# Unread products of constants on TensorE between the last expert pair and the first attention stream

## What is computed

```python
x = x + tanh(g_xattn[0]) * L0_xattn(layernorm(x), ctx)
x = x + tanh(g_ffn[0]) * L0_ffn(layernorm(x))      # 64 routed experts, top 4, and 2 shared ones
x = x + tanh(g_xattn[1]) * L1_xattn(layernorm(x), ctx, ctx)   # 32 query heads of 8, 8 key heads
x = x + tanh(g_ffn[1]) * L1_ffn(layernorm(x))      # causal attention of 16 heads, then gate, up, down
...
```

## Time and profile before

| | us |
|---|---|
| median of 3 launches | 1212.7 (1212.69 to 1216.48) |
| the profiled launch, its own time | 1211.12 |
| its span, first to last instruction | 1209.3 |
| TensorE busy | 1038.0 (86%) |
| VectorE busy | 722.9 (60%) |
| ScalarE busy | 523.0 (43%) |
| GpSimd busy | 308.2 (25%) |

### The profile page before, as it was taken

How to read it: one execution, slowest core, us unless ns; L and a number is a source line. 1 busy time by engine, 2 the same in 40 slices (tenths; PEclk the granted TensorE clock), 3 DMA queues, 4 the chain that set the end, 5 groups by cost and what they waited for, 6 DMA issues and landing times.

```text
span 1209.3 us, 18846 instructions
## 1 busy us (share of the span) xinstructions
PE 1038.0 (86%) x6621; PEld 660.5 (55%) x6621; DVE 722.9 (60%) x1630; ACT 523.0 (43%) x881; POOL 308.2 (25%) x618
## 2 busy tenths in 40 slices
PE   6399999999999788887889899962566978999997
PEld 4378888888887333333556337342223434556575
DVE  6965544544447568767655124487796665684744
ACT  3332222222243676665545411334553644544643
POOL 3024343434435555335331200010312200000000
PEclk9589999999999789899999999995767889999999
DMA  5202111121450000000000300020000000000000
GB/s 147 54 14 51 41 45 46 41 50 39 121 161 1 1 3 3 2 2 3 2 3 4 122 1 1 0 53 0 1 2 1 3 2 1 1 10 1 9 9 10
DMA packets 62461, 32.10 MB, mean 27 GB/s; under 512 B 47121, under 2 KB 61089, under 8 KB 62129
## 3 DMA queue, kind: packets, MB, share of 16 engines
q1 hardware_dynamic: 62384, 31.10, 9.6%
HBM read 29.64 MB, written 1.05 MB: 25 GB/s over the span
## 4 chain that ended last, share of the span: by engine, by line
PE 74%; DVE 17%; ACT 4%; issue 3%; POOL 1%; DMA 1%; POOLq 0%; DVEq 0%; SPq 0%; ACTq 0%; PEldq 0%
PE bank L780 16%; PE bank L806 8%; PE bank L915 4%; PE bank L1204 3%; PE bank L1388 3%; PE bank L1030 2%; PE bank L1133 2%; PE bank L998 2%; PE bank L1405 2%; PE bank L1390 2%; PE bank L960 2%; DVE mx L2379 2%; PE bank L1184 2%; PE bank L1220 1%; PE bank L1392 1%
## 5 line engine op out<-in xcount | busy, mean ns | idle before, releaser
L2379 DVE TENSOR_REDUCE mx<-bank 128x2 f32<-128x512 f32 (+1 forms) x176 | 117.7, 689 | 74.9 <-PE bank L1133 37.9
L1799 ACT ACTIVATE prob<-bank 128x512 f32<-128x512 f32 x176 | 103.2, 599 | 84.3 <-PE bank L1184 56.2
L1567 ACT ACTIVATE hhi<-hh 128x512 fp32r<-128x512 f32 x72 | 45.6, 633 | 156.1 <-DVE hh L2215 143.0
L2211 DVE TENSOR_TENSOR hu<-bank,sg 128x512 f32<-128x512 f32 x64 | 44.3, 692 | 92.1 <-PE bank L780 92.1
L780 PE MATMUL bank<-xh,wh 128*128 128x512 f32 x288 | 91.8, 400 | 0.3 <-DVE hh L2215 0.3
L780 PE MATMUL bank<-xh,wl 128*128 128x512 f32 x288 | 90.9, 396 | 0.0
L780 PE MATMUL bank<-xlo,wh 128*128 128x512 f32 x288 | 90.6, 396 | 0.0
L2203 DVE TENSOR_TENSOR hlo<-hh,hhi 128x512 fp32r<-128x512 f32 x72 | 57.2, 794 | 50.4 <-ACT hhi L1567 50.4
L2802 POOL TENSOR_TENSOR wl<-wraw,wh 128x512 fp32r<-128x512 f32 x72 | 81.6, 1133 | 13.0 <-POOL wh L2799 13.0
L1645 ACT ACTIVATE sg<-bank 128x512 f32<-128x512 f32 x72 | 43.1, 598 | 64.0 <-PE bank L780 64.0
L2799 POOL CAST wh<-wraw 128x512 fp32r<-128x512 f32 x72 | 37.1, 515 | 102.6 <-issue 51.8
(11 more groups left out here) (466 smaller groups left out, 2223.0 us busy)
## 6 DMA issues: line engine op xcount, KB each, us to landing
wraw<-in_L_ffn_wg_dram SPq DMA_DIRECT2D x64, 64.0 KB, 2.2
wraw<-in_L_ffn_wu_dram SPq DMA_DIRECT2D x64, 64.0 KB, 2.4
wraw<-in_L_ffn_wd_dram SPq DMA_DIRECT2D x32, 128.0 KB, 2.5
l_raw<-in_L_ffn_w_dram SPq DMA_DIRECT2D x2, 1024.0 KB, 6.6
mun<-in_L_ffn_mu_dram SPq DMA_DIRECT2D x1, 2048.0 KB, 7.5
xs<-in_x_dram SPq DMA_DIRECT2D x2, 512.0 KB, 4.5
w1s<-in_L_ffn_W_dram SPq DMA_DIRECT2D x2, 512.0 KB, 8.1
stage<-in_L_ffn_W_in_base_dram SPq DMA_DIRECT2D x1, 1024.0 KB, 8.1
```

The lines of the kernel that those rows point to most:

```text
L1567: return act.activation(dst, src, ACT.Copy, scale=scale)
L1799: act.activation(t.prob[k][:, :], bank[3 + n % 2][:, :], ACT.Exp).then_inc(S("probs"), 1)
L2211: tt(hu[k % 2][:, :], bank[4 + (n + 1) % 4][:, :], sg[k % 2][:, :], ALU.mult).then_inc(once("up_used"), 1)
L2379: V.reduce_max(out_, bank[n % 3][:, :].rearrange("p (h t) -> p h t", h=heads), AX, negate=True)\
```

## The change

A helper that makes `n` products of the constant `sel` with itself (96 rows, 128 x 512, bfloat16) into a bank that is free then. It counts no semaphore, and nothing reads the bank before it is written again. It is called at four points: 4 products after `wa`; 4 ahead of `turn_queries(0, 0)`; 2 ahead of `turn_keys(0, 1)`; and at each of the eight steps of slot -1 two, behind a wait for all of `prep_done`. That makes 4 + 4 + 2 + 16 = 26 products.

```diff
+            def keep_clock(k, n):
+                for _ in range(n):
+                    mm(bank[k][:, :], sel[:, 0, :], sel[:, 0:4, :], start=True, stop=True, skip_group_check=True)
...
             last.then_inc(once("wa_made"), 1)
+            keep_clock(5, 4)
             pe.wait_ge(once("batch_cleared"), 1)
             pe.wait_ge(once("experts_out"), 2 * HALVES)
...
                             q0, q1, k0, k1 = turning_steps(stream, s)
+                            if (stream, s) == ("A", 0):
+                                if k == q0:
+                                    keep_clock(2, 4)
+                                if k == 7:
+                                    keep_clock(2, 2)
                             if k == q0:
                                 turn_queries(s, 0)
...
                             for g in PREP_AT.get((sl, k), ()):
                                 prepare(g)
+                            if sl == -1:
+                                pe.wait_ge(once("prep_done"), len(PREP + PREPB))
+                                keep_clock(5, 2)
```

## The result

The changed kernel took 1218.9 us (median; 1208.91 to 1225.48) against 1212.7 before: ratio 1.004, 95% interval [1.0024, 1.0057]. It is 0.4% slower, outside my range of 1205.7 to 1214.5. The profiled launch took 1218.97, its span 1217.2.

A forecast was written before the change was run, and what follows sets the result against it. PE at half clock was taken as the bound over slots -2 to 0; -2.3 up to slot -1's end and -1.4 in slot 0 made -3.7, less 0.2: -3.5, so 1209.2 us from 1212.7, 8-in-10 range 1205.7 to 1214.5.

The forecast's parts named there:

- What bounds it: Stream A, slots -2 to 0: clock at half for 20.5 us, with PE the bound in slots -2 and 0.
- The price of one product: Each added 512-column product behind others: 0.215 us of PE at full clock, 0.43 at half.
- The step at full clock: Slot -1: tile 0.21 plus products 0.43 makes 0.64 us of PE a step, level with VectorE's 0.61.
- Slot -1: With the clock full, the turning of maxima at its end comes at 417.2 to 417.5 against 419.77: -2.3 up to there.
- Slot 0: With the clock full it takes near 7.0 us in place of 8.43: -1.4, between -1.0 and -2.1.
- The clock stays full: Likeliest case: granted clock 1.00 in 400 to 425, time 1209.2 us; chance 0.52.
- Rival 2: Slot -1: clock isn't won back, the sixteen products run at half and are the bound; +5.4, 1218 us; chance 0.07.
- slot -2's term: Slot -2 at full clock: VectorE's reductions run back to back and end at 409.85 in place of 411.75, -1.9 us.
- Rival 1: Clock falls all the same in slot -2 and comes back in slot -1; 1212.6 to 1213.9 us; chance 0.27.
- Rival 3: Later in stream A: further low stretches go too, up to 1.7 us each; -7, 1205.7 us; chance 0.14.
- the lead is kept: From slot 1 on nothing changes, so the -3.7 us won by then lasts to the end of the stream.

The follow-up runs named there:

- e3: The changed kernel plus five products in the 1.21 us idle stretch ahead of slot -2's first tile: 1210.21 us, ratio 0.9992.
- e1: The changed kernel without its part in slot -1 (ten products at three points, no wait for prep_done): 1212.72 us, ratio 0.9983.
- e6: The changed kernel with its wait for prep_done in slot -1 but without the sixteen products there: 1213.31 us, ratio 0.9997.
- e7: The changed kernel with one float32 product of winT a step in slot -1 in place of two bfloat16 ones of sel: 1221.25 us, ratio 1.0058.
- e10: e5 plus the wait for prep_done and four products in slot -1 ahead of the turning of maxima 0, none behind the tiles: 1212.56 us, ratio 1.0002.
- e5: e1 plus the five products of e3 in the 1.21 us idle stretch; nothing in slot -1: 1212.08 us, ratio 0.9981.
- e2: The changed kernel with only its slot -1 part (the wait and sixteen products), none at the three earlier points: 1219.67 us, ratio 1.0042.
- e11: The kernel before plus three float32 products of winT in idle stretches, in place of all of the change's products: 1215.92 us, ratio 1.0029.
- e4: The changed kernel with slot -1's sixteen products made of ternary weights w1qT in place of sel: 1215.96 us, ratio 1.0016.
- e9: e3 with one product a step in slot -1 in place of two: 1213.39 us, ratio 1.0016.

## Why the prediction was wrong, point by point

**What bounds it.** Right: the low stretch over slots -2 to 0, PE as the bound in slot -2. Held at full clock, maxima 2 came 3.5 us earlier (e3), and I had summed -3.7. It is close in part by two errors that cancel (below). Two readings of the slices were wrong, and nothing rests on them: there is a third low place, a 5 from 30 to 60 us, and the longer valley begins near 816 us, not 750.

**The price of one product.** Right: the second of two adds 1.04 - 0.61 = 0.43 at half clock and, at full, 0.61 - 0.39 = 0.22 by the rows above and the earlier trace rows. That is the price behind a product of the same kind. Between the tiles of slot -1 it was 0.55 at half clock (8.75 / 16). Ten of the 26 are hidden, as forecast: e1 isn't slower. So is the wait (e6).

**The step at full clock.** Mis-sized: I took 0.21 for the tile and so 0.64 a step; e3's steps take 0.86 (416.83 - 415.97): 0.54 for the two products (416.51 - 415.97) and 0.32 for the tile, where I had 0.43 and 0.21. At half clock it is 0.96 and 0.54, where I had 0.86 and 0.43. Tiles that follow each other take less than a tile between products; in the kernel before PE made three of them (two records each) at half clock in 1.03 us, 0.34 each:

```profile
414.81 1.03 PE L1133 MATMUL bank<-kTx,qT 48*128 48x256 bf16 x6
```

Slot -1 gave back 0.5 us in place of winning 0.4. Slot 0 won 2.1 in place of 1.4, and covered it.

**The step that failed** is the choice of the likeliest case: "The clock stays full: 0.52" and "Rival 2: 0.07". By the mean clock it was held in 3 launches of 20 and 2 of 11. It failed in two places. The first is slot -2's term, -1.9: I let the ten products ahead of it hold the clock, and gave no reason why they should with the 1.21 us still empty. In both traces of the change the clock fell about 1 us into slot -2 (404.4), and maxima 0 was 1.4 late in place of 1.9 early. The second is slot -1, where I expected the clock back. My ground for 0.07 was that "these are the longest products in this place, and PE has no idle among them". PE had none in slot -1, and the clock stayed at half from 404.4 to 431.7. I had read the falls as answers to idle stretches, and so took gapless PE for a rising clock. Against that stood a row that I had quoted myself: 405 to 410, PE busy 5.00, clock 0.55, and no rise for 16 us, though with idle of 1.08 and 0.99 us on the way.

The Trainium skill (TensorE: Matmul & The Clock Gate, Part 1) has the throttle released by sustained activity of PE. Here PE was busy for 19.9 of the 20 us from 405 to 425 at 0.50; the measurement decides, and busy time as the trace counts it is not enough.

**Rival 2's price** was right in kind and low: +5.4, from sixteen products at 0.43 less 1.5 of idle. The account says +6.7: +1.4 up to maxima 0, and +5.2 from there to maxima 1 (12.0 us in place of 6.8). What was low is the price of a product among the tiles, 0.55 in place of 0.43, so 8.75 in place of 6.9; the idle hid more than I had allowed, 2.2 in place of 1.5. Together that is 6.6, and 0.1 was lost in slot -2. The medians of the first series differ by 6.2.

**Rival 1** (the clock comes back in slot -1) occurred in no trace with bfloat16 products of sel. With float32 products it did (e7), at more than it won.

**Rival 3's** warning, that later falls move, was borne out with the other sign: in e10. And "the lead is kept" was not: e3's 3.5 us became 4.7 by the end of stream A and 2.3 by the span's end, e5's 4.4 and e10's 0.9 at the end of stream A became a lag.

**What is shown**: the sixteen products of slot -1 cost the time (e1, e2, e6), because they run at half clock in most launches (the traces of the change, of its repetition and of slot -1 alone each have some 27 us of it; for the launches without a trace it is read from time and mean clock). **What stays open**: what of PE's work brings the clock back. In the 13 traces with a low stretch in slots -2 to 0 it ended each time during a run of float32 products or within 1.6 us behind one, the added ones of winT in e7 and in the first of e11's two, `weighted` in all others; in no trace did it end behind bfloat16 work alone. But the float32 products don't do it each time: in e7 the rise came only as the fourth began, and in e4 and e9 the first `weighted` passed without one. And `weighted` stands at a fixed place, so only e7 and e11 speak for the float32 work itself. Ternary bfloat16 products gave mixed times. Rows, bits and zeros of the operands weren't varied one at a time. Nor was it tried to put work into slot -2, where PE at full clock has no room.

By the ratios no version beats the kernel before by more than 0.2% (e3's median is 3.4 us lower, but three of its 12 launches are long): e5, 0.9981 [0.9963, 0.9999], and e1, 0.9983 [0.9964, 1.0002].

## What to carry to other kernels

Filler work on an engine whose clock can halve has two prices, and the chance must be put on which one it will meet: in an idle stretch, at full clock, it was free (the first ten); behind each item of paced work it made TensorE the bound at both clocks, 0.86 us a step at full and 1.50 at half, against VectorE's 0.61. And work put between items that used to follow each other costs more than its own length (0.55 for 0.43). Ask first whether the filler will be there before the clock has fallen; once it has, filler only adds to the bound. And read from the trace whether busy PE has ever brought the clock back with work of that kind; a row of 5.00 busy at 0.50 says that being busy alone needn't.

## What was not expected of the hardware

- PE can be busy without a gap and stay at half clock: 15.00 of 15 us from 405 to 420 in the changed kernel, with transposes, products of 48 rows and bfloat16 products of 96 x 512.
- The clock can fall from full with PE busy 4.72 of 5 us, the only idle being 0.28 us (e9).
- With float32 products of 128 x 512 in slot -1 it came back after 13.7 us (e7), and behind a single one after 3.4 us (e11), where the change needed 27 us and the first `weighted`. That it is the float32 work isn't shown.
- One kernel's launches fall in groups with different mean clocks: 1209 us at 0.929 and 1219 at 0.914 to 0.916 for the change. A single trace shows one of them.
- A lead of 2.9 us at 425 us was lost by the end of the span (e10), 2.0 of it in the rest of stream A at a mean clock of 0.93 against 0.95: where the work stood otherwise in time, other later stretches ran at half.
- The part of the span behind stream A, which nothing here changes, takes 535.8 to 541.5 us from one traced launch to another. Whether a shift of the work or chance decides it isn't shown.
